# Row scaling of the experts and the last stages: from VectorE's two-step operation to one ScalarE activation with a bias column, in a two-layer decoder

## What is computed

```python
def _layernorm(x, axis=-1, eps=1e-05):
    m = jnp.mean(x, axis=axis, keepdims=True)
    v = jnp.var(x, axis=axis, keepdims=True)
    return (x - m) / jnp.sqrt(v + eps)
...
x = x + _L0_attn_ref(_layernorm(x), ...)     # self attention
x = x + _L0_xattn_ref(_layernorm(x), ...)    # attention over 8 x 128 context rows
x = x + _L0_ffn_ref(_layernorm(x), ...)      # 8 experts of rank 16 with softmax gates
x = x + _L1_attn_ref(_layernorm(x), ...)     # self attention, 32 query and 8 key heads
x = x + _L1_xattn_ref(_layernorm(x), ...)    # attended context rows, one head
x = x + _L1_ffn_ref(_layernorm(x), ...)      # product with a sign matrix, scaled
```

## Time and profile before

| | |
|---|---|
| median of three runs | 1005.76 us |
| the three runs | 1005.76, 1007.0, 999.32 us |
| the profiled execution, time on the device | 1003.03 us |
| its span in the trace | 1001.3 us |
| its mean granted TensorE clock | 0.969 of full speed |
| TensorE busy | 911.1 us (91%) |
| VectorE busy | 851.4 us (85%) |
| ScalarE busy | 635.1 us (63%) |
| POOL busy | 684.1 us (68%) |

### The profile page before, as it was taken

The page is one execution under the profiler, slowest core; times in us unless marked ns, Lnnn a source line. Parts: engine busy times, 40 slices in busy tenths (PEclk is TensorE's granted clock), DMA queues, the critical chain, the costliest instruction groups (busy, mean ns, idle before and its releaser), DMA issues. The chain is left out here.

```text
span 1001.3 us, 21553 instructions
## 1 busy us (share of the span) xinstructions
PE 911.1 (91%) x6504; PEld 465.7 (47%) x6504; DVE 851.4 (85%) x2090; ACT 635.1 (63%) x1786; POOL 684.1 (68%) x689
## 2 busy tenths in 40 slices
PE   5789998799989999999999999999768898999977
PEld 2344554344434554555555455554334454555543
DVE  7998998679975889999999999999679887677785
ACT  4687888743444666766666676666444378788551
POOL 5798998778764666676666666666267588565583
PEclk9789999889999999999999999999979999999999
DMA  9698998966543575655555555655433499877566
GB/s 351 127 200 152 166 169 176 198 129 127 117 85 95 120 118 119 119 126 126 126 115 119 119 127 119 127 123 126 110 100 81 90 175 159 145 140 125 108 147 148
DMA packets 384304, 136.32 MB, mean 136 GB/s; under 512 B 369760, under 2 KB 370400, under 8 KB 381792
## 3 DMA queue, kind: packets, MB, share of 16 engines
q1 hardware_dynamic: 384224, 135.39, 66.1%
HBM read 42.01 MB, written 2.10 MB: 44 GB/s over the span
## 5 line engine op out<-in xcount | busy, mean ns | idle before, releaser
L157 PE MATMUL bank<-w_hi,hT 128*128 128x512 f16 (+2 forms) x1024 | 323.3, 372 | 12.8 <-DVE w_lo L383 3.7
L157 PE MATMUL bank<-w_lo,hT 128*128 128x512 bf16 (+2 forms) x512 | 189.1, 372 | 0.0
L157 PE MATMUL bank<-w_hi,small 128*128 128x512 f16 x512 | 162.9, 379 | 7.7 <-DVE small L1551 7.7
L157 PEld LDWEIGHTS bank<-w_hi,hT 128*128 128x128 f16 (+1 forms) x1024 | 100.6, 99 | 120.2 <-issue 21.9
L1377 POOL TENSOR_TENSOR small<-small,mhalf 128x4 f32<-128x4 f32 x64 | 64.4, 1007 | 130.1 <-DVE small L974 129.9
L664 POOL TENSOR_TENSOR big<-big 128x512 f16<-128x512 f32 x96 | 116.2, 1217 | 32.2 <-DVE big L940 18.0
L1478 ACT ACTIVATE small<-small 128x128 f32<-128x128 f32 x256 | 98.7, 390 | 0.0
L157 PE MATMUL bank<-w_lo,small 128*128 128x512 bf16 x256 | 97.1, 379 | 0.0
L1393 POOL TENSOR_TENSOR w_lo<-stage,w_hi 128x512 bf16<-128x512 f32 x64 | 85.9, 1342 | 1.1 <-ACT w_hi L1514 1.1
L157 PE MATMUL bank<-small,big 128*128 128x17 f16 (+2 forms) x960 | 79.4, 213 | 7.8 <-issue 2.0
L824 ACT ACTIVATE big<-bank,small 128x128 f32<-128x128 f32 x256 | 71.9, 383 | 18.6 <-DVE small L929 18.3
(11 more groups left out here) (208 smaller groups left out, 2192.9 us busy)
## 6 DMA issues: line engine op xcount, KB each, us to landing
stage<-in_weights SPq DMA_DIRECT2D x16, 1024.0 KB, 6.2
stage<-in_weights SPq DMA_DIRECT2D x64, 256.0 KB, 2.9
big<-big SPq DMA_TRANSPOSE x168, 3.3
small<-in_ctxT SPq DMA_DIRECT2D x2, 1024.0 KB, 8.5
big<-in_ctx SPq DMA_DIRECT2D x2, 1024.0 KB, 5.6
out<-x SPq DMA_DIRECT2D x8, 256.0 KB, 2.4
big<-in_vectors SPq DMA_DIRECT2D x5, 256.0 KB, 11.3
x<-in_x SPq DMA_DIRECT2D x2, 512.0 KB, 4.7
```

The costliest lines, as they stand in the source:

```text
L157: last = nc.tensor.matmul(out, lhs(a, c), rhs(b, c), start=start and n == 0, stop=stop and n == 3 * chunks - 1)
```

## The change

The mean is no longer subtracted by VectorE. VectorE makes a column of 128 numbers, -mean x root, in one small step (`shift`), and ScalarE makes x x root + column with one activation (`Identity` with a scale column and a bias column). The column takes the place of variance + eps in memory, which is no longer needed then. The statistics of row b get a wait: for the scaling of row b - 2.

```diff
@@ class TurnedRows
+        self.shift_by = self.ve
...
     def stats(self, dve, b):
         nc, i = self.chip.nc, b % 2
+        after(dve, self.z_ready, b - 1)
         nc.vector.bn_stats(self.st[i], self.chip.x[:, b * D:(b + 1) * D]).then_inc(self.measured, 1)
...
-    def scale(self, dve, b):
+    def shift(self, dve, b):
         i = b % 2
         dve.wait_ge(self.rooted, b + 1)
-        after(dve, self.lo_ready, b - 1)
-        self.chip.nc.vector.tensor_scalar(self.z[i], self.chip.x[:, b * D:(b + 1) * D], self.mv[i][:, 0:1],
-                                          self.rs[:, i:i + 1], ALU.subtract, ALU.mult).then_inc(self.z_ready, 1)
+        self.chip.nc.vector.scalar_tensor_tensor(out=self.shift_by[:, i:i + 1], in0=self.mv[i][:, 0:1], scalar=-1.0,
+                                                 in1=self.rs[:, i:i + 1], op0=ALU.mult, op1=ALU.mult
+                                                 ).then_inc(self.shifted, 1)
+
+    def scale(self, act, b):
+        i = b % 2
+        act.wait_ge(self.shifted, b + 1)
+        after(act, self.lo_ready, b - 1)
+        self.chip.nc.scalar.activation(self.z[i], self.chip.x[:, b * D:(b + 1) * D], ACT.Identity,
+                                       bias=self.shift_by[:, i:i + 1], scale=self.rs[:, i:i + 1]).then_inc(self.z_ready, 1)
@@ Experts.vector (and the same for out, first and second)
-        if what == "in_z":
-            self.rows_in.scale(dve, n)
+        if what == "in_shift":
+            self.rows_in.shift(dve, n)
@@ Experts.scalar (and the same for out, first and second)
+        if what == "in_z":
+            self.rows_in.scale(act, n)
@@ SECOND_ORDER, tensor (first words; all lists of both tables are new)
-        key_0_0 key_1_0 key_2_0 gates_0_0 base_0_0 key_3_0 key_4_0 gates_1_0 share_turn_0_0 key_5_0 up_0_0 base_1_0
+        key_0_0 key_1_0 key_2_0 gates_0_0 base_0_0 key_3_0 base_1_0 share_turn_0_0 key_4_0 up_0_0 gates_1_0 up_1_0
@@ END_ORDER, tensor (one line)
-        p_turn_7_7 bias_1_0 pv_5_7 pv_6_7 pv_7_7 out_0_6 out_1_6 out_2_6 out_3_6 last_scores_0_0 last_scores_1_0
+        bias_0_0 pv_4_7 pv_5_7 out_0_6 pv_6_7 pv_7_7 bias_1_0 out_1_6 out_2_6 out_3_6 last_scores_0_0 last_scores_1_0
```

More of the change, by code:

```diff
@@ L1617, in __init__ @@
         self.mv = [mv[:, i * 2:(i + 1) * 2] for i in range(2)]
-        self.measured, self.var, self.rooted, self.z_ready, self.hi_ready, self.lo_ready = (
-            sem(f"{name}_{n}") for n in ("measured", "var", "rooted", "z", "hi", "lo"))
+        self.measured, self.var, self.rooted, self.shifted, self.z_ready, self.hi_ready, self.lo_ready = (
+            sem(f"{name}_{n}") for n in ("measured", "var", "rooted", "shifted", "z", "hi", "lo"))
         self.turned = [sem(f"{name}_turned{i}") for i in range(2)]
@@ new lines @@
+        p_hi_5_0 max_0_1 p_lo_4_0 max_1_1 out_stats_7_0 max_2_1 p_hi_0_1 p_lo_7_0 out_shift_6_0 max_3_1 max_4_1 v_hi_0_1
+        q_hi_0_2 o_take_0_0 q_hi_1_2 v_hi_1_1 max_5_1 out_shift_7_0 o_take_1_0 max_6_1 k_hi_0_2 p_lo_1_1 max_7_1
+        p_lo_4_1 p_hi_5_1 max_0_2 o_take_0_1 v_hi_0_2 max_1_2 p_hi_0_2 p_lo_7_1 q_hi_0_3 max_2_2 max_3_2 max_4_2
+        v_hi_1_2 q_hi_1_3 p_lo_1_2 o_take_1_1 max_5_2 k_hi_0_3 max_6_2 x_add_0_0 p_hi_5_2 max_7_2 p_lo_4_2 max_0_3
+        o_take_0_2 max_1_3 p_hi_0_3
@@ L1733 @@
+        p_turn_6_1 out_turn_6_0 p_turn_0_2 out_turn_7_0 q_turn_0_3 p_turn_2_2 p_turn_3_2
     """,
@@ L1929, in scalar @@
             self.background.split_hi(act, n)
+        if what == "in_z":
+            self.rows_in.scale(act, n)
         if what == "in_hi":
             self.rows_in.hi(act, n)
+        if what == "out_z":
+            self.rows_out.scale(act, n)
         if what == "out_hi":
@@ L1978, in vector @@
             self.rows_out.stats(dve, n)
-        if what == "out_z":
-            self.rows_out.scale(dve, n)
+        if what == "out_shift":
+            self.rows_out.shift(dve, n)
         if what in ("key_lo", "g_lo", "bias_lo"):
@@ new lines @@
+        last_second_shift_2_0 last_x_add_3_0 last_second_stats_3_0 last_x_add_4_0 last_second_stats_4_0
+        last_second_shift_3_0 last_prob_lo_5_0 last_out_0_0 last_second_shift_4_0 last_x_add_5_0 last_max_7_0
+        last_second_stats_5_0 last_prob_lo_6_0 last_prob_lo_7_0 last_out_1_0 last_second_shift_5_0 last_x_add_6_0
+        last_x_add_7_0 last_second_stats_6_0 last_second_stats_7_0 last_second_shift_6_0 last_out_2_0 last_out_3_0
+        last_second_shift_7_0 last_out_4_0 last_out_5_0 last_out_6_0 last_out_7_0
@@ L2104 @@
+        last_store_3_0 last_second_turn_7_0 last_store_4_0 last_store_5_0 last_store_6_0 last_store_7_0
     """,
@@ L2233, in step @@
                 nc.scalar.activation(deep(ch, b), cst[:, b * D:(b + 1) * D], ACT.Copy).then_inc(ctx_hi, 1)
+            if what == "first_z":
+                first.scale(act, b)
             if what == "first_hi":
                 first.hi(act, b)
+            if what == "second_z":
+                second.scale(act, b)
             if what == "second_hi":
@@ L2254, in step @@
                 first.stats(dve, b)
-            if what == "first_z":
-                first.scale(dve, b)
+            if what == "first_shift":
+                first.shift(dve, b)
             if what == "max":
@@ L2275, in step @@
                 second.stats(dve, b)
-            if what == "second_z":
-                second.scale(dve, b)
+            if what == "second_shift":
+                second.shift(dve, b)
             if what == "out":
```

172 lines of the change are left out of this document (83 added, 89 removed).

## The result

The changed kernel takes 1009.67 us in the median of 20 runs (1003.57 to 1013.39), beside 1005.62 us for the kernel before in as many (999.32 to 1009.74). The ratio is 1.0034, with a 95% interval of 1.0021 to 1.0047: it is slower by a third of a per cent, 4 us. The forecast was 997 us, and the result lies just outside the range of 987 to 1008. In what follows, ratios leave out one execution of e14 (3146.52 us) and one of e15 (1327.18 us) that ran in a slower state of the chip.

What follows compares the result with a forecast made beforehand. VectorE was taken to hold up TensorE in the experts' rows and last stages. Gains of 5.6 and 3.2 us less 1.3 for a table load gave 7.5 us, so a median of 997 us, range 987 to 1008.

Steps and rivals of the forecast that it cites:

- Part 1: Experts' rows and last stages: 32 scalings leave VectorE, shifts of 0.61 us replace them; 5.6 and 3.2 us won.
- rival 2: Experts' rows and last stages: the stall only moves to the shift; 2.7 us won, 1000.5 to 1003 us; chance 0.17.
- Part 2: All 32 rows: ScalarE takes the scalings at some 0.78 us each and has room everywhere, least in the last stages.
- Part 3: Last stages: `last_soft` moves ahead of the first exp, so a table load stands at that exp and costs 1.3 us.
- Part 4: New order: attention's last product starts earlier, and the context load with it, perhaps giving back about 1 us; counted as nothing.
- Part 5: Row statistics wait for ScalarE's scaling two rows before, and each scaling waits for a shift; both priced at nothing.
- Rival 3: Rows out of the experts: ScalarE stands waiting, 17 us on top, 1012.5 us or 1015 as a median; chance 0.13.

Runs made afterwards that it cites:

- e14: Changed kernel with one-input shift and old experts' lists, but new lists for VectorE, ScalarE and POOL behind `up_7`: 0.9981 of before.
- e15: Changed kernel with one-input shift and the old experts' lists, new end lists kept, a repeat run: 0.9955 of before.
- e1: Kernel before with the new operations and waits (two-input shift, scaling on ScalarE) put into its old lists: 1.0024 of before.
- e5: Kernel before with its old lists and the new operations, the shift having one tensor input: 0.9953 of before.
- e4: Changed kernel with `last_soft` moved back behind the last exp and one output step two places later: 1.0059 of before.
- e7: Changed kernel with one-input shift and the old experts' lists, new end lists kept, first run: 0.9938 of before.
- e3: Changed kernel with the shift written with one tensor input and the root as per-partition scalar, both new lists kept: 0.9980 of before.
- e12: Changed kernel with old experts' lists, new end lists and one-input shift, the shift made by POOL behind its root: 0.9981 of before.

## Why the prediction was wrong

**Part 1, the shift's price.** The mechanism was right: a two-input step is held up by POOL. The size was not. 0.61 us was the mean of another chain; in the experts' rows the shift took 0.92 us. In the piece shown it follows POOL's root, and POOL's split starts as the root ends; the prediction named this under rival 2 and then weighed it too little. In the last stages it took 0.53 us. What the stall costs the kernel was further off: the sum has 2.3 us for it (7.07 + 4.0 us unstalled against 5.6 + 3.2), and e1 against e5 gives 0.71%, 7.1 us.

**Part 1, what VectorE's time is worth.** This is the step that failed most: "8.63 - 5 x 0.61 = 5.6 us less on VectorE, under the 7.07 us that TensorE can get back", and 3.2 us more in the last stages. It took VectorE's old time in a stretch, less the new instruction, for time won by the kernel, one for one. In after the way from the first statistics to the first maximum got 0.4 us longer, not 5.6 shorter. Even with the stall gone (e5) it got 1.9 us shorter, VectorE lost 3.7 us instead of 7.6, and the kernel won 4.7 us where the same reckoning gives 11.1. The stall belongs to POOL's splits and not to the scaling: take its victim away, and another step stands there (the share chain from 10.0 to 13.2 us in e5, with the lists unchanged). That is rival 2 in a wider form than it was written: the stall changes its owner not only to the shift, but to the neighbourhood. Its price was still too kind, 1000.5 to 1003 us; the operations alone came out at 1.0024.

**Part 2, ScalarE's scaling.** Right: 0.78 us was given, 0.81 measured, and ScalarE had the room (19.76 of 37 us in the experts' rows).

**Part 3, the table load.** Its place and length were right. Its price of 1.3 us at the exp finds no support: without it the kernel is no faster (e4), and the chain of after doesn't pass there. The reason isn't the one in the clause "or nothing if the exp's maximum is late anyway": in the timelines of after the exp begins 1.6 us behind its maximum (959.02 to 960.62 us) and TensorE stands 1.84 us for it, but a turned row is later still. That the load in `soft` may cost something was left out.

**Part 4, the order.** "I take nothing" was wrong where it wasn't looked at. The context load isn't early (220.3 us behind the first statistics of the experts' stage in after, 216.7 before), and the end lists do nothing that shows, as priced. The experts' lists cost 0.25 to 0.5% with the unstalled shift, and in the halves tried the cost lies behind `up_7`, the last of the experts' products, where nothing was counted because TensorE was nearly full there. An engine that is nearly full can win little, but it can lose.

**Part 5, the new waits.** Priced at nothing, and partly wrong. ScalarE waits 16.4 and 9.9 us for shifts in after, and VectorE's statistics wait 1.9 us for ScalarE in after and 5.2 us in e5; what either costs by itself no run tells. Rival 3, ScalarE as the engine that stands, gave 1012.5 to 1015 us. The result is nearest to it, but not by its mechanism: the one-input shift, which leaves ScalarE's list as it is, takes the loss away.

The sum made anew from the runs, in us (0.1% is 1 us; each measured term is good to 2 or 3 us, and the last two can't be told apart):

| term | prediction | runs |
|---|---|---|
| operations without a stall | -11.1 | -4.7 (e5) |
| the stall of the shift | +2.3 | +7.1 (e1 against e5) |
| table load | +1.3 | not told apart |
| the orders, with the table load | 0 | +1.0 (after against e1) |
| sum | -7.5 | +3.4 |

The two terms of part 1 make up the whole miss of 10.9 us: 6.4 us for what VectorE's time is worth and 4.8 us for the stall.

## What to carry to other kernels

A stall that a neighbour engine causes isn't removed with the instruction that shows it: count what stands there next. A step that makes one column from two columns is better written with one tensor input and a per-partition scalar than with two tensors; with more elements than one the one-input form stalled here too. Idle time of the waiting engine is a bound of the gain and no estimate: taking 33 us of scalings from VectorE, in stretches that it fills, was worth 4 to 6 us at best here. And a new order is a change of its own: measure it apart from the operations. The version that keeps the old experts' lists, takes the new end lists and the one-input shift (one kernel, run as e7 and e15) beats both kernels: 1000.73 and 1002.45 us, ratios 0.9938 and 0.9955.

## What was not expected of the hardware

The same product of two 128x1 columns takes 97 to 215 ns with the second column as a per-partition scalar, and up to 2046 ns with it as a tensor while POOL works, though it reads two elements per partition and writes one. And the step with one tensor input and 128x2 elements, which has hardly more work, takes 157 to 1008 ns in the same execution of e3. On POOL this small step takes 343 ns in the mean in the experts' rows and 267 ns at the end, where VectorE takes 201 and 207 ns (e12, e3). An activation from SBUF with a bias column and a scale column takes 0.81 us, 0.13 more than one from a bank with a bias column alone. And the runs of one kernel on one core spread over 1%, so the profile of a single execution can't place a loss of 0.4%; the readings of the order above rest on ratios for that reason.
